# Last stage of a four-layer gated block on one core: part of the second additions moved from VectorE to GpSimd, fewer scalings on ScalarE, two pairs of semaphores made one

## What is computed

```python
x = x + jnp.tanh(g_xattn[i]) * attention_i(_layernorm(x), ctx)
x = x + jnp.tanh(g_ffn[i])   * ffn_i(_layernorm(x))
```

```python
out_e = jnp.einsum('ecf,efh->ech', hid, W_out)
gathered = out_pad[e_flat, l_flat].reshape(S, K, h)      # K = 2 outputs per token
y = (gathered * gates[..., None]).sum(axis=1)
```

## Time and profile before

| what | value |
|---|---|
| median of three runs | 1162.79 us (1162.28 to 1166.61) |
| span of the profiled execution | 1186.5 us |
| its own time beside the span | not given apart; the span is 23.7 us longer than the median of the runs |
| TensorE busy | 1029.6 us, 87% of the span |
| VectorE busy | 753.8 us, 64% |
| ScalarE busy | 495.1 us, 42% |
| GpSimd busy | 361.0 us, 30% |
| last stage, first load issued to end of span | 1162.4 to 1186.5 us |

### The profile page before, as it was taken

One profiled execution on the slowest core, in us unless ns is written; L12 is line 12 of the kernel. 1 busy time (PEld: TensorE's weight loads), 2 busy tenths in 40 slices (PEclk: granted clock), 3 DMA queues, 4 the chain that ended last, 5 costly groups with the idle time before them and its releaser, 6 DMA issues.

```text
span 1186.5 us, 17708 instructions
## 1 busy us (share of the span) xinstructions
PE 1029.6 (87%) x6335; PEld 619.7 (52%) x6342; DVE 753.8 (64%) x2234; ACT 495.1 (42%) x953; POOL 361.0 (30%) x406
## 2 busy tenths in 40 slices
PE   8999999985699987999999999999998873699870
PEld 6356666553444445436766666665454432366650
DVE  2657677788876667866766655556677566433334
ACT  2655555553344432553233333333444330444534
POOL 0060000012422456123352312004235546256561
PEclk7999999995799998999999999999999885899995
DMA  7083000030000002000015334440000001501016
GB/s 189 10 287 116 1 1 1 1 73 16 1 2 1 1 16 99 1 0 1 1 37 109 73 73 102 99 87 1 2 13 26 29 28 43 197 28 36 30 39 220
DMA packets 36871, 62.01 MB, mean 52 GB/s; under 512 B 6033, under 2 KB 21112, under 8 KB 35954
## 3 DMA queue, kind: packets, MB, share of 16 engines
q1 hardware_dynamic: 32178, 52.40, 16.3%
q0 software_dynamic: 4608, 8.50, 2.2%
HBM read 40.47 MB, written 21.45 MB: 52 GB/s over the span
## 4 chain that ended last, share of the span: by engine, by line
PE 59%; issue 16%; DVE 15%; ACT 4%; DMA 3%; POOL 1%; SPq 1%; another core or an unknown queue 0%; DVEq 0%; POOLq 0%; ACTq 0%
PE bank L1170 7%; PE bank L581 6%; PE bank L441 5%; PE bank L1186 5%; PE bank L484 5%; PE bank L644 3%; PE bank L412 3%; PE bank L470 2%; PE bank L477 2%; ACT att L1408 2%; DVE nmax L2127 2%; PE bank L600 2%; DVE xw L2006 1%; DMA big_a<-gates 1%; PE bank L945 1%
## 5 line engine op out<-in xcount | busy, mean ns | idle before, releaser
L1170 PE MATMUL bank<-big_b 128*128 128x512 f32 x288 | 135.8, 596 | 0.0
L2127 DVE TENSOR_REDUCE nmax<-bank 128x16 f32<-128x1024 f32 x64 | 78.3, 1224 | 55.6 <-PE bank L587 28.8
L1732 POOL TENSOR_SCALAR xn<-xw,mean,rstd 128x128 f32<-128x128 f32 x62 | 49.7, 811 | 184.4 <-DVEq L2705 90.0
L1902 POOL DMA_INDIRECT expert_outs<-big_a,big_b x80 | 77.9, 974 | 70.1 <-DVE big_a L2779 45.2
L1629 ACT ACTIVATE att<-bank 128x512 f32<-128x512 f32 (+1 forms) x72 | 43.0, 597 | 134.8 <-PE bank L1170 132.4
L1186 PEld LDWEIGHTS bank<-big_b,att 128*128 128x128 f32 (+1 forms) x576 | 72.9, 191 | 31.7 <-issue 19.1
L2642 DVE TENSOR_TENSOR att<-att,bank 128x512 f32<-128x512 f32 (+1 forms) x72 | 49.2, 683 | 57.7 <-PE bank L1186 54.9
L1893 POOL DMA_INDIRECT expert_rows<-xw,big_b x64 | 63.6, 994 | 68.5 <-DVEq L2225 51.7
L1408 ACT ACTIVATE att<-bank 128x1024 f32<-128x1024 f32 x64 | 62.0, 1021 | 45.3 <-PE bank L623 41.2
L1186 PE MATMUL bank<-big_b,att 128*128 128x128 f32 (+1 forms) x576 | 77.9, 278 | 3.4 <-DVE xw L2006 2.1
L2006 DVE SCALAR_TENSOR_TENSOR xw<-bank,tg,xw 128x128 f32<-128x128 f32 (+2 forms) x80 | 42.9, 536 | 54.5 <-PE bank L484 42.7
(11 more groups left out here) (423 smaller groups left out, 2186.7 us busy)
## 6 DMA issues: line engine op xcount, KB each, us to landing
big_a<-gates SPq DMA_DIRECT2D x14, 1024.0 KB, 9.7
expert_rows<-big_b SPq DMA_DIRECT2D x1, 5240.0 KB, 19.7
expert_outs<-big_b SPq DMA_DIRECT2D x1, 4096.0 KB, 31.3
big_a<-expert_outs SPq DMA_DIRECT2D x6, 512.0 KB, 7.8
big_a<-expert_rows SPq DMA_DIRECT2D x1, 2620.0 KB, 14.1
big_a<-in_mask SPq DMA_DIRECT2D x2, 1024.0 KB, 11.6
big_b<-in_w_in SPq DMA_DIRECT2D x1, 2048.0 KB, 8.0
out<-xw SPq DMA_DIRECT2D x8, 256.0 KB, 2.4
```

Source lines behind the costliest of these rows:

```text
L1170: mm = nc.tensor.matmul(bank[2 * (n % 3) + k][:, :], w13[:, k, c * 128:(c + 1) * 128], xnT_all[:, g * GW:(g + 1) * GW], start=True, stop=True)
L1902: nc.gpsimd.indirect_dma_start(outs3, bass.IndirectOffsetOnAxis(numbers3[:, ex, i:i + 1].bitcast(u32), 0), xs[:, ex, i, 0:D], None, bounds ...
L2127: nc.vector.tensor_reduce(nmax[:, j], psum[:, 2048:3072].rearrange("p (h t) -> p h t", t=T), AX.X, MAX, negate=True).then_inc(s.free, 1)
```

## The change

1. In the last stage, GpSimd gets a new function at the end of its queue, `second_adds`: for the groups 1 to 6 it waits for `k3.scaled` and `k3.added` and adds the scaled output 1 to x with one tensor_tensor of 128x512, which raises the new semaphore `k3.summed`.
2. VectorE does the second addition only in the groups 0 and 7 (`DVE_LAST`). In the others it goes on to the next group after the first addition, which raises `k3.added`. The first addition is now the four-instruction form in all groups.
3. ScalarE scales output 1 alone in all groups: 32 instructions where there were 40.
4. SyncE waits for `k3.added` in the groups 0 and 7 and for `k3.summed` in the others, before it stores a group. The order of the stores is the same.
5. The pairs `q_o`/`r_o` and `q_o_read`/`r_o_read` become one pair, `ffn_o` and `ffn_o_read`, which layer 0 counts from 1 to 8 and layer 1 from 9 to 16. Every wait is for the same event as before.

```diff
-        q_done, q_xT, q_xT_evac, q_o, q_o_read = sem("q_done"), ..., sem("q_o"), sem("q_o_read")
+        q_done, q_xT, q_xT_evac = sem("q_done"), sem("q_xT"), sem("q_xT_evac")
+        ffn_o, ffn_o_read = sem("ffn_o"), sem("ffn_o_read")
...
-        r_o, r_o_read = sem("r_o"), sem("r_o_read")
...
-        SCALED_GROUPS = (2, 5)
+        DVE_LAST = (0, 7)
...
             for g in range(NG):
-                sp.wait_ge(k3.added, g + 1)
+                if g in DVE_LAST:
+                    sp.wait_ge(k3.added, g + 1)
+                else:
+                    sp.wait_ge(k3.summed, g + 1 - sum(last < g for last in DVE_LAST))
                 sp.dma_start(out[:, TPG * g:TPG * g + TPG, :], x[:, TPG * g:TPG * g + TPG, :]).then_inc(dma_x, 16)
...
-                        pe.wait_ge(r_o_read, g)
+                        pe.wait_ge(ffn_o_read, NG + g)
...
-                    for k in (0, 1) if g in SCALED_GROUPS else (1,):
-                        for t in range(TPG * g, TPG * g + TPG):
-                            row = yt[:, k, t * D:(t + 1) * D]
-                            ins = nc.scalar.activation(row, row, ACT.Copy, scale=gate3[:, k, t:t + 1])
+                    for t in range(TPG * g, TPG * g + TPG):
+                        row = yt[:, 1, t * D:(t + 1) * D]
+                        ins = nc.scalar.activation(row, row, ACT.Copy, scale=gate3[:, 1, t:t + 1])
                     ins.then_inc(k3.scaled, 1)
...
+            def second_adds():
+                for g in (g for g in range(NG) if g not in DVE_LAST):
+                    tiles, columns = slice(TPG * g, TPG * g + TPG), slice(g * GW, (g + 1) * GW)
+                    pool.wait_ge(k3.scaled, g + 1)
+                    pool.wait_ge(k3.added, g + 1)
+                    nc.gpsimd.tensor_tensor(x[:, tiles], yt[:, 1, columns].rearrange("p (j d) -> p j d", d=D), x[:, tiles], ADD
+                                            ).then_inc(k3.summed, 1)
...
             from_slots()
+            second_adds()
...
                     dve.wait_ge(dma_span[RETURN_OF[g]], 16 + 16 * TOP3)
-                    if g in SCALED_GROUPS:
+                    for t in range(TPG * g, TPG * g + TPG):
+                        ins = stt(x[:, t], yt[:, 0, t * D:(t + 1) * D], gate3[:, 0, t:t + 1], x[:, t], MUL, ADD)
+                    if g in DVE_LAST:
+                        step(ins)
                         dve.wait_ge(k3.scaled, g + 1)
-                        ins = tensor_tensor(x[:, tiles], yt[:, 0, columns].rearrange("p (j d) -> p j d", d=D), x[:, tiles], ADD)
+                        tensor_tensor(x[:, tiles], yt[:, 1, columns].rearrange("p (j d) -> p j d", d=D), x[:, tiles], ADD
+                                      ).then_inc(k3.added, 1)
                     else:
-                        for t in range(TPG * g, TPG * g + TPG):
-                            ins = stt(x[:, t], yt[:, 0, t * D:(t + 1) * D], gate3[:, 0, t:t + 1], x[:, t], MUL, ADD)
-                    step(ins)
-                    dve.wait_ge(k3.scaled, g + 1)
-                    tensor_tensor(x[:, tiles], yt[:, 1, columns].rearrange("p (j d) -> p j d", d=D), x[:, tiles], ADD
-                                  ).then_inc(k3.added, 1)
+                        ins.then_inc(k3.added, 1)
```

More of the change, by code:

```diff
@@ L162, in flamingo_stack @@
         front_sems = Front()
-        q_done, q_xT, q_xT_evac, q_o, q_o_read = sem("q_done"), sem("q_xT"), sem("q_xT_evac"), sem("q_o"), sem("q_o_read")
+        q_done, q_xT, q_xT_evac = sem("q_done"), sem("q_xT"), sem("q_xT_evac")
+        ffn_o, ffn_o_read = sem("ffn_o"), sem("ffn_o_read")
         SHIFTED = 3
@@ L181, in flamingo_stack @@
         k3 = type("L3Routing", (), {name: sem(f"k_{name}") for name in (
-            "root", "marked", "ranks", "slots", "softmax", "scaled", "numbered", "normed", "added")})
+            "root", "marked", "ranks", "slots", "softmax", "scaled", "numbered", "normed", "added", "summed")})
         dma_fill, dma_slots, dma_span = sem("dma_fill"), sem("dma_slots"), [sem(f"dma_span{n}") for n in range(5)]
@@ L595, in turned @@
                         pe.wait_ge(s.v_evac, b + 1)
-                        pe.wait_ge(q_o_read, NG)
+                        pe.wait_ge(ffn_o_read, NG)
                     for c in range(2):
@@ L866, in turn @@
                     if not first:
-                        pe.wait_ge(q_o_read, g)
+                        pe.wait_ge(ffn_o_read, g)
                     if g == WARMED[0]:
@@ L872, in turn @@
                         mm = nc.tensor.matmul(dst, xnT[:, 0, j * 128:(j + 1) * 128], wq0T[:, :], start=True, stop=True)
-                    mm.then_inc(q_o, 1)
+                    mm.then_inc(ffn_o, 1)
                     if g in WARMED:
@@ L961, in outputs @@
                                               wout2T, start=True, stop=True)
-                    mm.then_inc(r_o, 1)
+                    mm.then_inc(ffn_o, 1)
                 def turn(g, first=False, second=False, last=False):
@@ L1130, in layer3_keys @@
                 if n:
-                    pe.wait_ge(r_o_read, NG)
+                    pe.wait_ge(ffn_o_read, 2 * NG)
                 nc.tensor.matmul(bank[(5, 7)[n]][:, :], wblk[:, 0], ctxT[:, n * 512:(n + 1) * 512],
@@ L2346, in output @@
                     dve.wait_ge(biased, g + 1)
-                    dve.wait_ge(q_o, g + 1)
-                    residual(1, TPG * g, bank[1][:, :], q_o_read, g + 1, tiles=TPG)
+                    dve.wait_ge(ffn_o, g + 1)
+                    residual(1, TPG * g, bank[1][:, :], ffn_o_read, g + 1, tiles=TPG)
                 ends, last = None, slice(NT - 2 * TPG, NT)
@@ L2453, in output @@
                 def output(g):
-                    dve.wait_ge(r_o, g + 1)
-                    residual(3, TPG * g, bank[7][:, :], r_o_read, g + 1, tiles=TPG)
+                    dve.wait_ge(ffn_o, NG + g + 1)
+                    residual(3, TPG * g, bank[7][:, :], ffn_o_read, NG + g + 1, tiles=TPG)
                 settled = slice(0, FIRST_SIMILAR)
```

## The result

The changed kernel took 1169.64 us, the median of 20 executions (1160.69 to 1171.87), against 1162.53 us for the kernel before (20 executions in turn with it on the same chip). The ratio is 1.0036, with a 95% interval of 1.0019 to 1.0054: some 4 us slower, where I had forecast 0.2 us less and a range up to 1165.4.

The account below looks back on a forecast made before the run. VectorE was taken to bound the last stage: 5.2 us freed, 5 us returned by exclusion with GpSimd, its end 1183.5 against 1183.74, so -0.2 us: 1162.6 us, range 1159.6 to 1165.4.

Parts of the forecast that it names:

- what bounds the stage: Last stage after group 2's data: VectorE sets the end; ScalarE's 24 instructions take 7.1 us and end at 1178.4.
- the exclusion: Groups 2 to 6: VectorE's first additions and GpSimd's additions, both reading SBUF, block each other; chance 0.6.
- L: Time each GpSimd addition of groups 2 to 6 takes from VectorE: 1.0 us taken, break-even 1.04.
- Rival A: VectorE's short first additions are hardly held up and stores become the bound: -3.1 us, 1159.7; chance 0.16.
- Rival B: Groups 2 to 6: GpSimd's additions cost VectorE their whole length and more, 1.26 us each; 1163.9 to 1164.4; chance 0.18.
- pile of additions: VectorE's back-to-back instructions keep GpSimd out, so group 6's addition ends beside group 7's: +0.5 us.
- 0.08 us of a wake-up: Part of the upper bound per GpSimd addition: 1.18 us of addition and 0.08 of wake-up, 1.26.
- group 1 and the data: Group 1's GpSimd addition costs nothing; VectorE's wait of about 1 us for groups 6 and 7's load vanishes if delayed.
- 2.75 us of store and end: Last term of the path, after VectorE's last addition: the last store and the end of the span.
- Rival D: Something elsewhere in the program moves through changed semaphores or code: 0.5% or more either way; chance 0.06.
- 5.8 us: Whole kernel: the difference a measurement can tell from no change, some 0.5%.
- two stores leaving together: Groups 6 and 7: if GpSimd's additions pile up, both stores leave at once, +0.5 us.

Follow-up runs that it names:

- e1_before_again: The kernel before against itself, no edit, on a slower chip: 1190.62 against 1190.75 us, ratio 0.9997 (0.9962 to 1.0031).
- e12_sems_again: The kernel before with only the semaphore pairs merged, last stage unchanged, run once more on another chip: ratio 1.0005 (0.9980 to 1.0031).

## Why the prediction was wrong

**Right: what bounds the stage.** From group 2's data on VectorE was busy without a gap in the changed kernel, and ScalarE ended 3.6 us before it (1159.94 against 1163.52).

**Right: the exclusion and its size.** I took L = 1.0 us per GpSimd addition, from the earlier trace rows, with VectorE's last addition 12.2 us after the data. It took 11.84: the 24 first additions lasted 11.12 us where 6.45 were worked out without GpSimd, so L = 4.67/5 = 0.93, within the 0.91 to 1.26 of the working. Rival A fell. The earlier trace rows was no evidence for it: I wrote that L2548 took its 0.35 us inside a GpSimd instruction, but it began 0.56 us into one of 0.79 and ended behind it. The trace of before had a better pair on the same lines. Here L2548 begins 0.08 us after the GpSimd instruction and takes 0.51 in place of 0.35:

```profile
577.21 0.80 POOL L1834 TENSOR_SCALAR xn<-xw,mean,rstd 128x128 f32<-128x128 f32 x1
577.29 0.51 DVE L2548 SCALAR_TENSOR_TENSOR big_a<-big_b,big_a 128x128 f32<-128x128 f32 x1
```

Rival B's L of 1.26 didn't occur either; nor did its pile of additions, as they started 1.9 to 2.0 us apart and took 1.18 us, only the first of the five 1.36. The 0.08 us of a wake-up in that 1.26 stand in no row; from group 6's last first addition (ended at 1160.80) to GpSimd's (1160.94) it took 0.14. Nor was the whole 1.18 us of an addition lost: that would have put VectorE's last addition 13.1 us after the data. In the row at 1160.98 VectorE's instruction ends 0.15 us after GpSimd's, though it takes 0.35 alone, so some 0.2 us of the two did overlap.

**Right, but not asked far enough: group 1 and the data.** Group 1's addition cost nothing on the path, and VectorE had no wait for data left in the groups 4 to 7.

**Wrong: the end of the path.** The step that failed is "2.75 us of store and end", together with this sentence on GpSimd's queue: "The new waits on its queue stand behind everything else it has, so nothing is queued behind them but the next additions." Behind them is the drain that closes the queue. In this program it ends 7.6 us after GpSimd's last instruction, and the change moved that instruction from 22.7 us ahead of VectorE's last addition to 1.4 us ahead of it. The term missing in the sum was: GpSimd's last addition, at about 1182 by my own working (group 7's work on VectorE still follows it), plus 7.6, plus 0.25 for the meeting of the engines: 1189.8 against an end at 1186.5, +3.3 us, 1166.1. The trace of before held the number; line 58's view has the drain of 13.5 us that ends at 1168.7. The timeline, from which I took the path, doesn't show drains. That they are 7.6 us after the last instruction, whichever that is, no row of before could say by itself; the drain there stands behind an indirect DMA alone.

**The rest of the miss.** The path gives +3.1 us, and the median came out 7.1 us above that of before while the ratio says 4.2. The ratio is the better measure, as a median jumps with how many executions lie at which clock: 14 of 20 of the changed kernel lay at the lower; how many of the kernel before did is not on record. Rival D (something elsewhere moves) got 0.06 and isn't needed for the 3.1 us; the semaphores alone gave 1.0022, 1.0002 and 1.0005, with 1 inside each interval. The 5.8 us that I said a measurement can tell from no change were too many: 20 executions of each tell 0.18%, 2 us.

**The range.** On the slow side it was made of L, of two stores leaving together and of 1 us for scatter. With the drain in the sum, 1166.1 would have been its centre; the median of 1169.64 lies 3.5 us above that too.

## What to carry to other kernels

When the last work of a program moves to another engine, the end of that engine's queue moves with it: look up what each queue still does after its last instruction in the trace of before, and add it. In this program the first drain of GpSimd behind its indirect DMAs takes 7.6 us; put one where GpSimd is idle, or give it nothing late. And before an elementwise addition is handed to GpSimd beside a VectorE that reads two inputs, compare what it costs VectorE by exclusion (0.93 us here) with what it costs it to do the addition (1.78 us less the 4 x 0.265 = 1.06 of the first additions, 0.72 us): the handover lost even before the drain.

## What the runs showed of the hardware that I had not expected

- A drain of GpSimd after indirect DMAs takes 7.6 us from its last instruction, in every run that had them (7.59 to 7.61), whether the DMAs ended just before or 21 us earlier; after one such drain the next ended less than 0.1 us after GpSimd's last instruction, and without indirect DMAs too. What is done in that time no trace here shows, nor was it tried whether it depends on the number of the DMAs.
- A GpSimd memset of 0.97 us beside VectorE's two-input instructions costs them nothing, an addition of 1.18 us costs them 0.93.
- The same program took 1162.5 us on one chip and 1190 us on another. They part in two stretches, those in which GpSimd issues its indirect DMAs. From the first to the last of the 64 to expert_rows it takes 127.7 us on the slower chip (`e1_before_again`) and 117.2 on a faster one (`e12_sems_again`); the matmuls of the experts (L1219 to L1243) run over 131 us against 119. Together that is 23 us, and the two spans differ by 21. From 1020 to 1120 us the granted clock is 0.98 in both traces, yet the slower one issues 439 matmuls and the faster 506. Why was not followed, and ratios are taken on one chip only.
